# Both MLP layers of a four-layer transformer kernel, from one fp32 product to three fp32r products of high and low parts

## The chip, the cores and the metric

The kernel runs on one core of a Trainium2 chip. The time is the device time of one execution in microseconds (us), lower is better; the median of the runs of a kernel is compared.

A core has five engines with an instruction queue each: TensorE (PE, matrix products into the accumulator memory PSUM), VectorE (DVE), ScalarE (ACT), GpSimd (POOL) and SyncE (SP, which issues the DMAs here). They meet at semaphores only.

## The reference

`x` and a context have 8 batches of 512 tokens of 256 features, all in fp32. Four layers follow one another; the stages that the change touches are the two MLPs, at the end of layer 0 and of layer 2:

```python
# layer 0                                        # layer 2, the same form
x = x + self_attention(ln1(x))                   # 16 heads of 16
x = x + cross_attention(ln2(x), ctx)
h = gelu(ln3(x) @ fc_w.T + fc_b)                 # 256 -> 1024, exact Gelu
x = x + h @ proj_w.T + proj_b                    # 1024 -> 256
```

Layer 1 is a cross attention with quantized weights, layer 3 a causal attention with heads of 64.

## The kernel before

Everything stays on the chip: `X` holds all 8 batches (128 partitions = tokens of a tile, 4 tiles a batch, 256 columns). The program runs eight stages in order: SELF0, CROSS0, MLP0, CROSS1, SELF2, CROSS2, MLP2, SELF3. Between some of them, the MLP stages among them, all engines wait on `x_done` for the last batch of the stage before (L886, L1074, L1373, L1596).

An MLP stage loops over `NB` = 8 batches. Its first and last batch are written out, the six between are a loop on each engine. The weights of a stage (`W_even`, 128 x 4096 fp32: 2048 columns for the first layer, `wf`, 2048 for the second, `wp`) are loaded during the stage before.

- PE (`mlp`, L710 to L744). `turn(b)` transposes the normalized batch, 4 transposes of 128x128 into each of the banks `LA` and `LB`. `batch(b)` makes the first layer: for each of `NF` = 8 chunks `f` of 128 hidden units two products over the 256 features (`NC` = 2 halves `c`, 512 columns each) into `FR[f % 4]`, one of four PSUM banks, after the wait for the Gelu three chunks back. Then come the transposes of the next batch, then the wait for all eight Gelus, then the second layer: 4 token tiles x 8 chunks, 256 columns a product, into `OV[0]` and `OV[1]`. The records name `FR` as MX and ST, and `h1T` as V, since it lies in the memory of V.
- ACT (`mlp`, L983 to L1004). `turned(b)` evacuates LA and LB into `hT` with the layer norm's scale and shift; for each chunk one Gelu with bias from PSUM into `h1T` (128 x 8 x 512).
- DVE (`mlp`, L1200 to L1214). The layer norm's statistics of batch b+1 (4 `bn_stats`, 4 `bn_aggr`), then for both halves of the second layer `add_to_x`, `X` plus the PSUM bank.
- POOL (`mlp`, L1515 to L1528). `layer_norm` of batch b+1: scale (L1399), power (L1401), centring (L1407), product (L1412) into `XH`, the centring once the transposes of the batch before are done; then `add_bias` for batch b (L1418) once `add_to_x` is done. That operation also counts up `x_done`.

In time, a batch's second layer ends, DVE adds, POOL adds the bias and makes the next layer norm, while PE is in the first layer of the next batch.

fp32r is the 4-byte type that PE multiplies in rounded form. The attention stages use it for scores: `stk` holds high and low parts of queries and keys on 48 or 50 partitions, and SELF2 adds its mask by two products of `identr` with `mask_hi` and `mask_lo` on 128 partitions (L667 to L669). The two parts of that mask are made by L1367 (copy to fp32r) and L1369 (subtraction). All products are recorded under L529, all transposes here under L539. `hi` and `lo` (128 x 2 x 512 fp32r) belong to the attention stages and are free in an MLP stage, as is `stk`.

Of the kernel before, what the change touches and what calls it, by code (L numbers as in the profile page):

```python
# [8 lines left out]
F32 = mybir.dt.float32  # L9
# [6 lines left out]
P = 128  # L16
NB = 8
# [43 lines left out]
def program(nc, x_in, ctx_in, ctx_rows_in, masks_in, shapes_in, cols_in, rows_in, wts, out):  # L61
# [12 lines left out]
    with es:  # L74
# [69 lines left out]
        columns3 = Pr[:, 0, 0:2, :].rearrange("p a (k m) -> p (a k) m", m=P)  # L144

# [14 lines left out]
        def P3(qt, h):  # L160
# [34 lines left out]
            sem("fc_full"), sem("gelu_done"), sem("pr_full"), sem("pr_evac"), sem("ml_full"), sem("ml_evac"))  # L195
        bias3, later3_set, cols3_in, k3_apart = sem("bias3"), sem("later3_set"), sem("cols3_in"), sem("k3_apart")
# [61 lines left out]


# [267 lines left out]
        def _(pe):  # L527
# [182 lines left out]
            def mlp(s):  # L710
                m = MLP_NO[s]
                wf = W[s % 2][:, 0:2048].rearrange("p (c o) -> p c o", c=NC)
                wp = W[s % 2][:, 2048:4096].rearrange("p (f o) -> p f o", f=NF)
# [7 lines left out]
                def batch(b, more):  # L721
                    MB = NB * m + b
                    pe.wait_ge(ml_evac, 2 * (MB + 1))
                    for f in range(NF):
                        wait(pe, gelu_done, NF * MB + f - 3)
                        for c in range(NC):
                            last = mm(FR[f % 4][:, :], wf[:, c, P * f:P * f + P], hT[:, c, :], c == 0, c == NC - 1)
                        last.then_inc(fc_full, 1)
                    if more:
                        turn(b + 1)  # L730
                    pe.wait_ge(gelu_done, NF * (MB + 1))
                    for j in range(2):
                        wait(pe, pr_evac, 2 * (MB - 1) + j + 1)
                        for t in range(2):
                            tok = slice(P * (2 * j + t), P * (2 * j + t) + P)
# [5 lines left out]
                batch(0, True)  # L741
                with pe.Fori(1, NB - 1) as b:
                    batch(b, True)
                batch(NB - 1, False)  # L744
# [161 lines left out]
        def _(act):  # L906
# [76 lines left out]
            def mlp(s):  # L983
                m = MLP_NO[s]

                def turned(b):
                    for c, bank in enumerate((LA, LB)):
                        act.wait_ge(ml_full, 2 * (NB * m + b) + c + 1)
                        nc.scalar.activation(hT[:, c, :], bank[:, :], ACT.Identity, **scale_shift(s, c)).then_inc(ml_evac, 1)

                def batch(b, more):
# [5 lines left out]
                    if more:  # L997
                        turned(b + 1)

                turned(0)  # L1000
                batch(0, True)
                with act.Fori(1, NB - 1) as b:
                    batch(b, True)
                batch(NB - 1, False)  # L1004
# [79 lines left out]
        def _(dve):  # L1084
# [115 lines left out]
            def mlp(s):  # L1200
                m = MLP_NO[s]

                def batch(b, more):
                    if more:
                        layer_norm_x(NB * s + b + 1, b + 1)
                    for j in range(2):
# [4 lines left out]
                batch(0, True)  # L1211
                with dve.Fori(1, NB - 1) as b:
                    batch(b, True)
                batch(NB - 1, False)  # L1214
# [173 lines left out]
        def _(pool):  # L1388
# [126 lines left out]
            def mlp(s):  # L1515
                m = MLP_NO[s]

                def batch(b, more):
                    if more:
# [3 lines left out]

                layer_norm(NB * s, xt(0, 0, NT))
                batch(0, True)
                with pool.Fori(1, NB - 1) as b:
                    batch(b, True)
                batch(NB - 1, False)  # L1528
# [173 lines left out]
```

## Time and profile before

| | us |
|---|---|
| median of 3 runs (4552.29 to 4562.95) | 4558.77 |
| the profiled execution, its own time | 4563.0 |
| MLP0 stage, from `x_done` to `x_done` | 245.0 |
| MLP2 stage | 245.1 |

The profile is one execution, taken by the hardware profiler. PE is the matmul unit, PEld its weight loads, which are recorded apart. A fp32 product has two matmul records and two loads, a fp32r product one of each. Matmuls are pipelined and a record is longer than the step to the next, so what counts is the distance from start to start. A load that is needed at once starts with its product; otherwise loads run ahead. PEclk (the granted clock) is the share of full speed at which TensorE ran: 1.00 is 2.4 GHz, 0.50 is 1.2 GHz. "Idle before" is idle time of an engine ahead of a group and what ended it. A line of the timeline that merges several instructions gives the start of the first and the time to the end of the last.

### The profile page before, as it was taken

To read this page: it belongs to the slowest core of one execution; us is meant where nothing else is said; L and a number is where in the kernel's file an instruction comes from. 1 tells how busy PE (TensorE), PEld (TensorE's weight loads), DVE (VectorE), ACT (ScalarE), POOL (GpSimd) and SP (SyncE) were. 2 spreads that over 40 slices of the span, in tenths; PEclk is the share of its full clock that TensorE was granted. 3 is DMA by queue.
4 is the path that set the end of the run, shared out by engine and by line. 5 is a ranking of instruction groups with operands and counts; after the bars stand their busy time and mean duration, and the time that the engine had idled before them with its cause. 6 is when DMAs were issued, how large, how long until landed. Compare 5 with 4: busy or idle time off the path is not lost. (4 is left out here: it accounts for less than half of the span.)

```text
span 4563.0 us, 63561 instructions
## 1 busy us (share of the span) xinstructions
PE 4206.8 (92%) x20178; PEld 2005.3 (44%) x20178; DVE 2460.5 (54%) x6321; ACT 2386.1 (52%) x5045; POOL 1642.4 (36%) x1661
## 2 busy tenths in 40 slices
PE   6988899999796999999999999999797999999998
PEld 3333333333464333333333333333464555555555
DVE  4555567775013777776666667776011544444443
ACT  2444456666221666666666666666221555555553
POOL 2332321111221111236556541110221766666664
PEclk7888889999897899999999999999798999999999
DMA  4433334442001444433222234442000000000000
GB/s 94 81 64 61 62 66 98 78 78 50 16 0 32 97 79 74 76 58 74 51 52 50 48 62 96 72 76 55 27 0 28 6 1 10 11 10 11 10 6 10
DMA packets 135470, 219.98 MB, mean 48 GB/s; under 512 B 42736, under 2 KB 45168, under 8 KB 133488
## 3 DMA queue, kind: packets, MB, share of 16 engines
q1 hardware_dynamic: 135152, 216.02, 24.0%
q8 instruction: 165, 2.70, 0.3%
q14 instruction: 153, 1.25, 0.1%
HBM read 59.69 MB, written 5.51 MB: 14 GB/s over the span
## 5 line engine op out<-in xcount | busy, mean ns | idle before, releaser
L967 ACT ACTIVATE Pr<-ST 128x512 f32<-128x512 f32 (+3 forms) x2392 | 1249.3, 563 | 990.3 <-PE ST L529 907.2
L529 PE MATMUL ST<-stk 50*128 50x512 f32 (+3 forms) x2560 | 1075.8, 471 | 98.9 <-ACT Pr L967 86.3
L1169 DVE TENSOR_REDUCE mx<-MX 128x1 f32<-128x512 f32 x1056 | 699.7, 683 | 251.4 <-PE MX L529 250.0
L529 PE MATMUL MX<-stk 48*128 48x512 f32 (+3 forms) x1760 | 753.6, 463 | 23.7 <-issue 11.9
L1548 POOL TENSOR_SCALAR Pr<-Pr,mx 128x128 f32<-128x128 f32 (+3 forms) x512 | 548.4, 1083 | 384.1 <-DVE mx L1307 384.1
L529 PE MATMUL OV<-Pr,V 128*32 128x512 f32 (+3 forms) x4784 | 649.9, 618 | 2.6 <-ACT Pr L967 1.5
L529 PEld LDWEIGHTS MX<-stk 48*128 48x128 f32 x1760 | 316.9, 195 | 614.6 <-issue 265.5
L529 PEld LDWEIGHTS ST<-stk 50*128 50x128 f32 x2560 | 441.8, 194 | 275.1 <-ACT Pr L967 233.9
L1421 POOL CAST mhl<-mx 128x16 fp32r<-128x16 f32 x160 | 31.6, 197 | 1121.2 <-DVE mx L1169 1078.1
L529 PE MATMUL OV<-stk 48*128 48x512 f32 (+3 forms) x800 | 366.6, 458 | 57.2 <-DVE mx L1169 45.3
L1169 DVE TENSOR_REDUCE mx<-OV 128x1 f32<-128x512 f32 x480 | 324.8, 677 | 65.0 <-PE OV L529 64.1
L1162 DVE CUSTOM_DVE_ANT_0 MX<-MX,W_even 128x512 f32<-128x512 f32 x352 | 244.4, 699 | 150.9 <-PE MX L529 124.1
L529 PEld LDWEIGHTS OV<-stk 48*128 48x128 f32 x800 | 156.6, 196 | 350.7 <-DVE mx L1169 224.8
L1499 POOL TENSOR_TENSOR Pr<-Pr,W_odd 128x512 f32<-128x512 f32 x172 | 220.3, 1282 | 177.5 <-ACT Pr L967 177.4
L1036 ACT ACTIVATE Pr<-MX,mx 128x128 f32<-128x128 f32 (+3 forms) x256 | 134.9, 527 | 263.9 <-DVE mx L1301 263.4
L1418 POOL TENSOR_TENSOR X<-X,brow 128x1024 f32<-128x1024 f32 (+1 forms) x56 | 132.0, 2357 | 378.7 <-DVE X L1108 378.7
L1166 DVE CUSTOM_DVE_ANT_0 MX<-MX,later 128x128 f32<-128x128 f32 (+3 forms) x352 | 174.2, 511 | 170.5 <-PE MX L529 168.1
L1108 DVE TENSOR_TENSOR X<-OV,X 128x512 f32 (+1 forms) x32 | 22.1, 691 | 428.0 <-PE OV L529 428.0
L1316 DVE COPY PT<-OV 128x128 f32<-128x128 f32 (+3 forms) x256 | 125.5, 490 | 222.6 <-PE OV L808 222.6
L1301 DVE CUSTOM_DVE_ANT_0 MX<-MX,sums 128x128 f32<-128x128 f32 (+3 forms) x256 | 126.9, 496 | 212.4 <-PE ST L529 208.3
L529 PE MATMUL OV<-W_even,V 128*128 128x256 f32 x1024 | 225.2, 381 | 1.6 <-ACT V L995 1.6
L1506 POOL TENSOR_SCALAR_AFFINE_SELECT Pr<-Pr 128x512 f32<-128x512 f32 x128 | 81.3, 635 | 376.7 <-ACT Pr L967 376.7
(144 smaller groups left out, 7198.3 us busy)
## 6 DMA issues: line engine op xcount, KB each, us to landing
stk<-hi SPq DMA_DIRECT2D x640, 128.0 KB, 4.0
stk<-lo SPq DMA_DIRECT2D x320, 128.0 KB, 3.9
misc<-misc SPq DMA_DIRECT2D x160, 128.0 KB
sums<-spread SPq DMA_DIRECT2D x80, 256.0 KB
misc<-in_ctx_t SPq DMA_DIRECT2D x24, 512.0 KB, 6.6
W_even<-in_w SPq DMA_DIRECT2D x4, 1024.0 KB, 5.2
W_even<-in_w SPq DMA_DIRECT2D x2, 2048.0 KB, 10.5
XH<-in_ctx_rows SPq DMA_DIRECT2D x8, 512.0 KB, 3.9
```

Of the source, the lines that this page charges most:

```text
L529: return nc.tensor.matmul(o, l, r, start=start, stop=stop)
L967: nc.scalar.activation(pr_buffer(s, u, i)[:, h, q0:S], ST[h % 2][:, q0:S], func).then_inc(ex_done, 1)
L1036: nc.scalar.activation(P3(qt, h)[:, 0:k_n], S3[h][t % 2][:, 0:k_n], ACT.Exp, bias=low3[:, qt, h:h + 1], scale=-1.0, accum_out=total3[:, qt ...
L1162: nc.vector.tensor_tensor_reduce(bank[:, :], bank[:, :], mask_q[:, qt, :], 1.0, -3.0e38, ALU.add, ALU.max, m).then_inc(mx_red, 1)
L1166: nc.vector.tensor_tensor_reduce(bank[:, 0:k_n], bank[:, 0:k_n], later0[:, S - k_n:S], 1.0, -3.0e38, ALU.add, ALU.max, m).then_inc(mx_red, 1)
L1169: nc.vector.tensor_reduce(m, bank[:, :], AX.X, ALU.max).then_inc(mx_red, 1)
L1301: nc.vector.tensor_tensor_reduce(bank, bank, later3[:, S - k_n:S], 1.0, 3.0e38, ALU.add, ALU.min, low3[:, qt, h:h + 1]).then_inc(low3_done, 1)
L1316: nc.vector.tensor_copy(to, TP3[1][:, 0:P * (qt + 1)].rearrange("p (k n) -> p k n", n=P)).then_inc(tp3_evac[1], 1)
L1418: nc.gpsimd.tensor_tensor(xt(b, 0, NT), xt(b, 0, NT), bias, ALU.add).then_inc(x_done, 1)
L1499: nc.gpsimd.tensor_tensor(tile, tile, mask_k[:, i % 4, :], ALU.add).then_inc(pool_masked, 1)
L1506: nc.gpsimd.affine_select(tile, tile, [[0, G], [1, P]], ALU.is_ge, 0.0, 0, -1).then_inc(cleared, 1)
L1548: nc.gpsimd.tensor_scalar(tile, tile, inv3[:, qt, h:h + 1], None, ALU.mult).then_inc(nm3_done, 1)
```

## The change

All products of both MLP stages are taken from high and low parts. High part: the value rounded to fp32r; low part: value minus high part, rounded too. A product w·h becomes w_hi·h_hi + w_lo·h_hi + w_hi·h_lo in one PSUM sum; w_lo·h_lo is left out.

- PE: 6 products a chunk in the first layer (48 a batch in place of 16 in fp32), 96 in place of 32 in the second. In each group the products with the low activations come last, behind a wait of their own (`ml_lo`, `h1_lo_done`). The wait for all Gelus at once is replaced by waits for each chunk's high and low part in the first token tile. In batch 0 there are also waits for the weights' parts.
- ACT: at the start of a stage the high parts of the weights in 8 pieces of 512 columns (`split_weights`); per batch each of LA and LB is now evacuated twice, to `hi` and to `hT`.
- DVE: at the start the weights' low parts; per batch `split_hidden` for each chunk (a copy to `h1_hi`, a wait for it, a subtraction to `h1_lo`) between the layer norm's statistics and `add_to_x`, and `low_turned` (two subtractions) ahead of `add_to_x`.
- POOL: the same operations.
- Memory: `w_hi` and `w_lo` lie in `stk`, `h1_hi` in `misc`, `h1_lo` in `Pr`. All four loops over batches are written out.

```diff
+        w_hi = stk[:, 16:24, :].rearrange("p a n -> p (a n)")
+        w_lo = stk[:, 24:32, :].rearrange("p a n -> p (a n)")
+        h1_hi = nc.alloc_sbuf_tensor_at("h1_hi", [P, NF, S], F32R, offset=misc_at)
+        h1_lo = nc.alloc_sbuf_tensor_at("h1_lo", [P, NF, S], F32R, offset=pr_at)
+        def weight_cut(k):
+            if k < 4:
+                return [(E * k + c * 1024, E) for c in range(NC)]
+            return [(2048 + 512 * (k - 4), 512)]
...
@@ PE, mlp
-                def batch(b, more):
-                    pe.wait_ge(ml_evac, 2 * (MB + 1))
+                def batch(b):
+                    pe.wait_ge(ml_hi, 2 * (MB + 1))
                     for f in range(NF):
+                        cut = slice(P * f, P * f + P)
                         wait(pe, gelu_done, NF * MB + f - 3)
+                        if b == 0 and f % 2 == 0:
+                            pe.wait_ge(wf_hi_done, 8 * m + f // 2 + 1)
+                            pe.wait_ge(wf_lo_done, 8 * m + f // 2 + 1)
                         for c in range(NC):
-                            last = mm(FR[f % 4][:, :], wf[:, c, P * f:P * f + P], hT[:, c, :], c == 0, c == NC - 1)
+                            mm(FR[f % 4][:, :], wf_hi[:, c, cut], hi[:, c, :], c == 0, False)
+                            mm(FR[f % 4][:, :], wf_lo[:, c, cut], hi[:, c, :], False, False)
+                        if f == 0:
+                            pe.wait_ge(ml_lo, 2 * (MB + 1))
+                        for c in range(NC):
+                            last = mm(FR[f % 4][:, :], wf_hi[:, c, cut], lo[:, c, :], False, c == NC - 1)
                         last.then_inc(fc_full, 1)
...
-                    pe.wait_ge(gelu_done, NF * (MB + 1))
+                    if b == 0:
+                        pe.wait_ge(wf_hi_done, 8 * (m + 1))
+                        pe.wait_ge(wf_lo_done, 8 * (m + 1))
                     for j in range(2):
                         wait(pe, pr_evac, 2 * (MB - 1) + j + 1)
                         for t in range(2):
                             for f in range(NF):
-                                last = mm(OV[j][:, E * t:E * t + E], h1T[:, f, tok], wp[:, f, :], f == 0, f == NF - 1)
+                                if j == 0 and t == 0:
+                                    pe.wait_ge(h1_hi_done, NF * MB + f + 1)
+                                mm(bank, h1_hi[:, f, tok], wp_hi[:, f, :], f == 0, False)
+                                mm(bank, h1_hi[:, f, tok], wp_lo[:, f, :], False, False)
+                            for f in range(NF):
+                                if j == 0 and t == 0:
+                                    pe.wait_ge(h1_lo_done, NF * MB + f + 1)
+                                last = mm(bank, h1_lo[:, f, tok], wp_hi[:, f, :], False, f == NF - 1)
                         last.then_inc(pr_full, 1)
@@ ACT, mlp
+                def split_weights():
+                    act.wait_ge(w_in[s], 16)
+                    for k in range(8):
+                        cut = weight_cut(k)
+                        nc.scalar.activation(w_part(w_hi, cut), w_part(W[s % 2], cut), ACT.Copy).then_inc(wf_hi_done, 1)
                 def turned(b):
                     for c, bank in enumerate((LA, LB)):
+                        nc.scalar.activation(hi[:, c, :], bank[:, :], ACT.Identity, **scale_shift(s, c)).then_inc(ml_hi, 1)
                         nc.scalar.activation(hT[:, c, :], bank[:, :], ACT.Identity, **scale_shift(s, c)).then_inc(ml_evac, 1)
@@ DVE, mlp
+                def weights_low():
+                    for k in range(8):
+                        cut = weight_cut(k)
+                        dve.wait_ge(wf_hi_done, 8 * m + k + 1)
+                        nc.vector.tensor_tensor(w_part(w_lo, cut), w_part(W[s % 2], cut), w_part(w_hi, cut).bitcast(F32),
+                                                ALU.subtract).then_inc(wf_lo_done, 1)
+                def low_turned(b):
+                    for c in range(NC):
+                        dve.wait_ge(ml_evac, 2 * (NB * m + b) + c + 1)
+                        nc.vector.tensor_tensor(lo[:, c, :], hT[:, c, :], hi[:, c, :].bitcast(F32), ALU.subtract).then_inc(ml_lo, 1)
+                def split_hidden(b, f):
+                    at = NF * (NB * m + b) + f
+                    dve.wait_ge(gelu_done, at + 1)
+                    nc.vector.tensor_copy(h1_hi[:, f, :], h1T[:, f, :]).then_inc(h1_hi_done, 1)
+                    dve.wait_ge(h1_hi_done, at + 1)
+                    nc.vector.tensor_tensor(h1_lo[:, f, :], h1T[:, f, :], h1_hi[:, f, :].bitcast(F32),
+                                            ALU.subtract).then_inc(h1_lo_done, 1)
+                def batch(b):
+                    if b + 1 < NB:
                         layer_norm_x(NB * s + b + 1, b + 1)
+                    for f in range(NF):
+                        split_hidden(b, f)
+                    if b + 1 < NB:
+                        low_turned(b + 1)
                     for j in range(2):
                         dve.wait_ge(pr_full, 2 * (NB * m + b) + j + 1)
                         add_to_x(b, j, OV[j][:, :].rearrange("p (t n) -> p t n", t=2), pr_evac)
                 layer_norm_x(NB * s, 0)
+                weights_low()
+                low_turned(0)
+                for b in range(NB):
+                    batch(b)
```

## Rows read from the trace of the kernel before

**Rows 1.** The page, part 1: busy us (share) x instructions.
```profile
PE 4206.8 (92%) x20178; PEld 2005.3 (44%) x20178; DVE 2460.5 (54%) x6321; ACT 2386.1 (52%) x5045; POOL 1642.4 (36%) x1661
```

**Rows 2.** Stretches: length, busy PE PEld DVE ACT POOL (count), PEclk, DMA share, GB/s.
```profile
1172.03:1417.00 244.97, 232.89 (x832) 154.10 (x832) 24.38 (x80) 56.17 (x81) 59.02 (x40) 0.97 0.02 6
1213.00:1385.08 172.08, 172.08 (x625) 114.57 (x624) 18.14 (x60) 41.00 (x60) 44.23 (x30) 1.00 0.00 0
3240.50:3485.60 245.10, 232.73 (x832) 154.13 (x832) 24.40 (x81) 56.17 (x81) 59.19 (x41) 0.97 0.02 9
```

**Rows 3.** Waits in MLP0: who <- for whom: total us, times, longest.
```profile
DVE X L1108 <- PE OV L529: 214.1, 16, 26.7
...
PE LA L539 <- POOL XH L1412: 10.5, 1, 10.5
```

**Rows 4.** Timeline of batch 1 of MLP0: start, us, engine, instruction, xcount.
```profile
1213.00 3.60 PE L529 MATMUL MX<-hT,W_even 128*128 128x512 f32 x8
...
1213.97 2.35 POOL L1418 TENSOR_TENSOR X<-X,brow 128x1024 f32<-128x1024 f32 x1 [28.72 <-DVE X L1108]
...
1215.12 0.36 DVE L1096 BATCH_NORM_AGGREGATE mv<-st 128x2 f32<-128x6 f32 x4
...
1216.43 3.60 PE L529 MATMUL ST<-hT,W_even 128*128 128x512 f32 x8
...
1217.92 1.90 POOL L1407 TENSOR_TENSOR XH<-X,mv 128x1024 f32<-128x1024 f32 x1 [0.29 <-POOL rstd L1401]
...
1226.73 0.60 PE L539 MATMUL LA<-ident,XH 128*128 128x128 f32 x4
1227.17 0.60 PE L539 MATMUL LB<-ident,XH 128*128 128x128 f32 x4
1227.77 0.91 PE L529 MATMUL OV<-W_even,V 128*128 128x256 f32 x3
```

**Rows 5.** Timeline of SELF2: the two mask products, the second one's load.
```profile
2306.00 0.50 PE L529 MATMUL ST<-stk,identr 128*128 128x512 f32 x1
...
2306.34 0.40 PE L529 MATMUL ST<-stk,identr 128*128 128x512 f32 x1
...
2306.11 0.19 PEld L529 LDWEIGHTS ST<-stk,identr 128*128 128x128 f32 x1
```

**Rows 6.** Timeline of SELF0, causal: fp32r products of 256 columns, a load.
```profile
180.54 0.33 PE L529 MATMUL MX<-stk 48*128 48x256 f32 x1
180.71 0.33 PE L529 MATMUL OV<-stk 48*128 48x384 f32 x1
...
180.59 0.19 PEld L529 LDWEIGHTS OV<-stk 48*128 48x128 f32 x1
```

**Rows 7.** Lines: durations min/median/max in ns; DVE operations from SBUF to SBUF.
```profile
L1219 DVE TENSOR_SCALAR W_odd<-W_odd x3: 416/427/622, 568.8 to 2608.0; 128x512 f32<-128x512 f32 x3
L1367 DVE CAST stk<-W_odd x1: 1222/1222/1222, 1936.9 to 1936.9; 128x2048 fp32r<-128x2048 f32 x1
L1369 DVE TENSOR_TENSOR stk<-W_odd,stk x1: 2291/2291/2291, 1938.2 to 1938.2; 128x2048 fp32r<-128x2048 f32 x1
```

**Rows 8.** Timeline, DVE beside POOL: program start and SELF2's end.
```profile
5.66 2.46 DVE L1352 CAST identr<-ident 128x128 fp32r<-128x128 f32 x1 [5.66 <-issue]
0.97 7.07 POOL L1582 MEMSET stk<- 32x4096 f32 x2
...
2608.01 0.62 DVE L1219 TENSOR_SCALAR W_odd<-W_odd 128x512 f32<-128x512 f32 x1
2607.08 1.27 POOL L1499 TENSOR_TENSOR Pr<-Pr,W_odd 128x512 f32<-128x512 f32 x1 [1.17 <-ACT Pr L967]
```

**Rows 9.** Timeline of MLP0: first product, last batch's second layer.
```profile
1181.28 0.78 ACT L989 ACTIVATE hT<-LB,cols 128x512 f32<-128x512 f32 x1
1182.11 5.89 PE L529 MATMUL MX<-hT,W_even 128*128 128x512 f32 x8 [0.87 <-ACT hT L989]
...
1399.76 14.08 PE L529 MATMUL OV<-W_even,V 128*128 128x256 f32 x64 [0.78 <-ACT V L995]
```

More of the change, by code:

```diff
@@ L257, in wq, with w_part @@
             return W[s % 2][:, 512 * m:512 * m + 512].rearrange("p (c o) -> p c o", c=NC)
+        def weight_cut(k):
+            if k < 4:
+                return [(E * k + c * 1024, E) for c in range(NC)]
+            return [(2048 + 512 * (k - 4), 512)]
+        def w_part(w, cut):
+            at, n = cut[0]
+            if len(cut) == 2:
+                return w[:, 0:2048].rearrange("p (c o) -> p c o", c=NC)[:, :, at:at + n]
+            return w[:, at:at + n]
         def stages(u):
@@ L711, in mlp @@
                 m = MLP_NO[s]
-                wf = W[s % 2][:, 0:2048].rearrange("p (c o) -> p c o", c=NC)
-                wp = W[s % 2][:, 2048:4096].rearrange("p (f o) -> p f o", f=NF)
+                wf_hi, wf_lo = (w[:, 0:2048].rearrange("p (c o) -> p c o", c=NC) for w in (w_hi, w_lo))
+                wp_hi, wp_lo = (w[:, 2048:4096].rearrange("p (f o) -> p f o", f=NF) for w in (w_hi, w_lo))
                 def turn(b):
@@ L996, in batch @@
                                              bias=cols[:, at:at + 1]).then_inc(gelu_done, 1)
-                    if more:
+                    if b + 1 < NB:
                         turned(b + 1)
+                split_weights()
                 turned(0)
[L1001 to L1004, printed above, removed]
+                for b in range(NB):
+                    batch(b)
             def layer3(s):
@@ L1201, in mlp, with batch @@
                 m = MLP_NO[s]
-                def batch(b, more):
-                    if more:
+                def weights_low():
[15 more added lines that the diff above has]
+                                            ALU.subtract).then_inc(h1_lo_done, 1)
+                def batch(b):
+                    if b + 1 < NB:
                         layer_norm_x(NB * s + b + 1, b + 1)
+                    for f in range(NF):
+                        split_hidden(b, f)
+                    if b + 1 < NB:
+                        low_turned(b + 1)
                     for j in range(2):
@@ L1210, in mlp @@
                 layer_norm_x(NB * s, 0)
[L1211 to L1214, printed above, removed]
+                weights_low()
+                low_turned(0)
+                for b in range(NB):
+                    batch(b)
             def scale_queries(s, w, scale):
@@ L1516, in mlp @@
                 m = MLP_NO[s]
-                def batch(b, more):
-                    if more:
+                layer_norm(NB * s, xt(0, 0, NT))
+                for b in range(NB):
+                    if b + 1 < NB:
                         layer_norm(NB * s + b + 1, xt(b + 1, 0, NT), ml_full, 2 * (NB * m + b + 1))
@@ L1522, in batch @@
                     add_bias(s, b)
[L1524 to L1528, printed above, removed]
             def layer3(s):
```

14 lines of the change are left out of this document (6 added, 8 removed).

## Prediction

> **What bounds the kernel now.** I read four views in this order. The page's busy line says TensorE (PE) is busy 92% of the span [rows 1], an average over eight stages, so it settles nothing for the two that change. The table by stretch gives those: the MLP stages last 245.0 and 245.1 us, PE busy 233 of each, and the six middle batches of the first show 172.08 us busy of 172.08 at granted clock 1.00 [rows 2]. There is no gap at all. The waits of that stage agree: DVE waits for PE for 214 us in all; PE's one long wait is 10.5 us for the first layer norm [rows 3]. So a batch costs what PE's instructions cost, 172.08 / 6 = 28.68 us, and there are 16. The timeline of one batch takes it apart [rows 4]. First layer: 8 records in 3.43 us (1213.00 to 1216.43), two records to an fp32 product, so 0.858 us for 512 columns, and 16 of them make 13.7. Eight transposes and the step to the second layer take 1.04 (1226.73 to 1227.77). Second layer: 64 records (32 products of 256 columns) take 13.8 (14.08 with the drain). Beside them ACT is busy 41.00 / 6 = 6.8 us, POOL 7.4 and DVE 3.0: all idle for most of a batch.
>
> **What the change does to PE.** One fp32 product (two records of 0.429 us at 512 columns) becomes three fp32r products of one record each. Their price is not in the MLP stages, so it comes from the nearest rows. 512 columns on all 128 rows: two mask products in attention start at 2306.00 and 2306.34; the first had to wait for its own weights, whose load takes 0.107 (the next load starts at 2306.11) [rows 5]. That leaves 0.232 us streamed, where half an fp32 record is 0.214. I take 0.234 with the step; 0.216, half a record with the step, is the other end. First layer: 8 chunks x 2 x 3 = 48 products, 48 x 0.234 = 11.2 us (10.4 at the fast end) against 13.7.
>
> 256 columns: a load of 128 columns now lies behind every 0.11 us of streaming. In the causal stage a load starts at 180.59 and its product at 180.71, 0.12 later, while the product before it (256 columns, recorded at 180.54 but with its weights there only at 180.59) streamed [rows 6]. The load ran beside the product and the pair took 0.12. The transposes are the other end: four loads and four products in 0.44 (1226.73 to 1227.17), 0.110 each [rows 4]. I take 0.12, as that row has the fp32r type. Second layer: 4 token tiles x 8 x 3 = 96 products, 11.5 us (10.5) against 13.8. With 0.95 for the transposes (the loop's own step left out) PE needs 11.2 + 0.95 + 11.5 = 23.7 us a batch (21.9 at the fast ends). The loops go as well: a batch is now written out.
>
> **What it adds elsewhere.** ACT: two more evacuations of 0.78 a batch [rows 9], 8.4 us in all, under PE's 23.7; they are queued behind the eighth Gelu and are needed only by the next batch, 11.5 us later: nothing. DMA: nothing. POOL's work stays at 7.4 us. DVE gets a copy and a subtraction for each of 8 hidden chunks. A one-input SBUF operation of 512 columns is 0.42 us, the fp32r copy of 2048 is 1.22, so 0.15 of each is fixed; the subtraction of 2048 is 2.29, so one of 512 is 2.14 / 4 + 0.15 = 0.69 [rows 7]; with the handover between them a chunk takes 1.09. Two low parts of the activations (1.4) come behind, hidden under the second layer. A batch's DVE work is 3.0 + 8.7 + 1.4 = 13.1 us, well under 23.7; a chunk's 1.09 is under PE's 1.40 a chunk. On busy time alone, DVE hides.
>
> It is the place that matters. The eight splits can't start before the two layer-norm steps of the next batch (DVE free 2.48 us after the batch's start, 1215.48 less 1213.00), and in just this time POOL works: bias 0.97 to 3.32, two small operations, centring 4.92 to 6.82, and a product of the same length [rows 4]. The trace shows that DVE and POOL hold each other up. At the start a cast of 128x128 took 2.46 us and ended 0.08 after POOL's memset, and a 0.42 us operation became 0.62 beside a POOL tensor_tensor that ended at 2608.35 [rows 8]. For the subtraction with two SBUF inputs beside POOL there is no row. Bounds: no hold-up, or a full one like the copy's. I take the full one, since the copy is the nearest row and both bring two SBUF streams into DVE at once.
>
> Turn by turn, from the batch's start (after a hand-over a copy needs 0.28, as in the 2608 row, a subtraction 0.55 by the same 0.14 off): POOL's bias to 3.3; copy 0 to 3.6; POOL's first small one to 3.8; subtraction 0 to 4.3; the second (about 1.0) to 5.3; copy 1 to 5.6; centring to 7.5; subtraction 1 to 8.1; POOL's product to 10.0 (before PE wants it at 11.2); copy 2 and subtraction 2 to 10.95; then five chunks of 1.09 alone, so the high part of the eighth chunk is there at 15.7. PE reaches the product that waits for it at 11.2 + 0.95 + 14 x 0.12 = 13.9. It waits 1.8, and then 82 products of 0.12 are left: 15.7 + 9.8 = 25.5 us a batch. The eighth low part (16.4) is not late, since PE asks for it 9 products later (16.8). If only the copies are held, the same count gives 14.4 for that high part and 24.2 a batch. If nothing is, 23.7.
>
> The Trainium skill ("SBUF — State Buffer", SBUF: two separate sides) says that DVE and GpSimd share one port pair as an exclusive lock for a whole instruction, taken by DVE also for two SBUF inputs against a GpSimd operation that reads SBUF. The rows on the copies agree (0.62 against 0.42); by that rule it would be 25.5, by busy time alone 23.7.
>
> **Start and end of a stage.** The first layer norm's 10.5 us on POOL is the one time when PE waits [rows 9]. ACT copies the weights' high parts there (eight of at most 0.78, from 1172.0), each ready ahead of DVE. DVE's 8 subtractions are interleaved with POOL's four operations, three or four ahead of POOL's end, 0.55 each: 2.0 us later, between 0 and 2.5. The first product then waits for both high evacuations, and a hidden copy to hT now stands between them: +0.78 (ACT 0.78 each; 1182.11 was right behind the second). I take 2.8 us a stage. The low activations are asked for four products later and are ready 1.5 later (0.78 and 0.69); the clock is low there (8 records in 5.89 us in place of 3.60 [rows 4, 9]), so four products last about as long. The last batch has no transposes and no layer norm: now 14.68 to the second layer (with 0.78 waiting for Gelu) plus 13.8 and some drain, 28.6 [rows 9]; afterwards 11.2 + 11.5 = 22.8 (the eighth high part at 12.6 is in time for 12.9). It saves 5.8.
>
> **Sum.** 14 batches x (28.68 - 25.5) = 44.5; 2 last ones x 5.8 = 11.6; less 2 x 2.8 = 5.6: 50.5 us. The profiled execution's own 4563.0 becomes 4512.5. It is at the top of the three runs, 4.2 above their median, so the forecast for the median is 4508 us.
>
> **Rivals.** (1) Little or no hold-up between DVE and POOL: 24.2 a batch gives 14 x 4.5 + 11.6 - 3 = 71 us, 4488; with 23.7, 78 us, 4480. For it: no row shows two-input operations colliding. Against: the copies do. (2) The products run at the fast ends, 0.216 and 0.110, and nothing is held up: 21.9 a batch, 14 x 6.8 + 2 x 7.7 - 3 = 108, 4451. Against: the two mask products of rows 5 start 0.34 apart, not 0.32. (3) Slower: the weight loads of the second layer become the bound. Before, a load of 0.19 lay behind 0.215 of streaming; now it lies behind 0.116. If it does not run beside the product, a step is 0.107 + 0.116 = 0.223, the second layer 21.4 us, a batch 33.6, and the kernel 16 x 4.9 + 3 = 81 us slower, 4640. It decides from a step of (28.68 - 12.15) / 96 = 0.172 on. Against: rows 4 and 6, where load and product overlap. The Trainium skill ("TensorE: Matmul & The Clock Gate", Measured speedup vs the span model) says that a load overlaps running matmuls only where the row groups differ. Here they never do; both layers would pay it, 38.6 a batch and about 4720 us. The trace speaks against it: full-row transposes with a load each follow every 0.110 us. (4) The hold-up is worse, or the one-pass product at 256 columns steps at 0.16 to 0.17 because of its waits (16 of them stand in the first token tile): 27.5 to 28.5 a batch, 4536 to 4550, no change at its end. Against: fulfilled waits at chunk boundaries cost nothing now (records step on at 0.43).
>
> **How the numbers follow.** Forecast with the full hold-up (4495 to 4525): 0.52. Rival 1 (4474 to 4495): 0.27. Rival 2 (under 4474): 0.08. Rival 4: 0.08, of it 0.03 within no change. Rival 3: 0.05. The range reaches from rival 1's lower end to some way into rival 4: 4466 to 4530; outside lie rival 2, rival 3 and most of 4, under 2 in 10. What a measurement can tell from no change is 0.2%, 9 us: faster 0.92, same 0.03, slower 0.05.
>
> **What would show it.** A middle batch of 25.5 us, not 23.7 or 28.7. First-layer products starting 0.232 to 0.236 apart, second-layer ones 0.12. One wait of PE a batch, some 1.8 us, in the first token tile of the second layer, for the high part of the eighth chunk. DVE copies and subtractions stretched to 1 to 2 us while POOL's bias and layer norm run, and 0.42 and 0.69 afterwards; POOL's product ending 10 us after the batch's start. Layers outside the MLP stages unchanged. Wrong would be: a step of 0.17 or more in the second layer, a clock under 1.00 in the middle batches, or a wait of PE on ACT.

## The result, and the profile after

| | before | after |
|---|---|---|
| median (range) | 4560.86 (4552.29 to 4577.34), 4 runs | 4483.74 (4481.09 to 4504.7), 4 runs |
| the profiled execution, span of its core | 4563.0 | 4479.3 |
| MLP0 / MLP2, from `x_done` to `x_done` | 245.0 / 245.1 | 208.4 / 208.5 |
| a middle batch | 28.68 | 24.36 |

The ratio of the times is 0.9839, 95% interval 0.981 to 0.9869. The kernel is 77 us (1.6%) faster by the medians, where 51 were forecast. All times below are in us.

The table by stretch of the kernel after (length, busy PE, PEld, DVE, ACT, POOL with counts, granted clock, DMA share, GB/s): MLP0, one middle batch, MLP2. It answers to [rows 2].

```profile
1177.60:1386.00 208.40, 192.25 (x1216) 173.38 (x1216) 136.76 (x232) 71.24 (x105) 67.88 (x40) 0.96 0.02 7
1238.46:1262.81 24.35, 23.79 (x154) 21.46 (x153) 16.50 (x28) 8.20 (x12) 8.61 (x5) 1.00 0.00 1
3191.30:3399.80 208.50, 192.31 (x1216) 173.43 (x1216) 136.76 (x233) 71.24 (x105) 67.88 (x40) 0.97 0.03 12
```

Each stage is 36.6 shorter, 73.2 together; the two profiled spans are 83.7 apart. The other 10.5 lie in the attention stages, whose code is the same. The batch is no longer all PE: it is busy 23.79 of 24.35, and DVE has gone from 3 to 16.5 us a batch, POOL from 7.4 to 8.6 with the same work.

The waits of PE on DVE from the start of MLP0 into its last batch (who on whom, total, times, longest; batches 1 to 6 have one of PE each):

```profile
PEld OV L549 <- DVE h_hi L1262: 5.7, 12, 0.8
PE OV L549 <- DVE h_hi L1262: 3.4, 6, 0.6
```

So there is one wait of PE a batch, on the copy to `h1_hi`. The timeline of batch 1 shows where. First PE (start, us, instruction, count): the first products of the first layer, the transposes, the first token tile of the second layer.

```profile
1214.09 1.09 PE L549 MATMUL MX<-hi,stk 128*128 128x512 f32 x4
...
1225.00 0.60 PE L559 MATMUL LA<-ident,XH 128*128 128x128 f32 x4
...
1225.79 2.17 PE L549 MATMUL OV<-stk,h_hi 128*128 128x256 f32 x14
1228.52 0.51 PE L549 MATMUL OV<-stk,h_hi 128*128 128x256 f32 x2 [0.56 <-DVE h_hi L1262]
1228.86 1.12 PE L549 MATMUL OV<-stk,h_lo 128*128 128x256 f32 x8
1229.82 2.08 PE L549 MATMUL OV<-stk,h_hi 128*128 128x256 f32 x16
```

The first layer starts at 1214.09 and the transposes at 1225.00: 48 products in 10.91, 0.2273 each. The transposes take 0.79 (to 1225.79). In the second layer 8 products take 0.96 (1228.86 to 1229.82), 0.120 each. Fourteen products would end at 1225.79 + 14 x 0.12 = 1227.47; the fifteenth runs at 1228.52, 1.05 late. The profile calls 0.56 of this idle, because the last record before it outlasts its step. Then DVE and POOL in the same batch:

```profile
1215.06 2.40 POOL L1486 TENSOR_TENSOR X<-X,brow 128x1024 f32<-128x1024 f32 x1 [17.26 <-DVE X L1152]
1216.49 1.26 DVE L1262 CAST h_hi<-V 128x512 fp32r<-128x512 f32 x1
1217.92 1.46 POOL L1469 TENSOR_TENSOR rstd<-rstd,mhalf 128x4 f32<-128x4 f32 x1
1218.39 0.42 DVE L1262 CAST h_hi<-V 128x512 fp32r<-128x512 f32 x1
1218.84 0.69 DVE L1264 TENSOR_TENSOR h_lo<-V,h_hi 128x512 fp32r<-128x512 f32 x1
1219.45 2.18 POOL L1475 TENSOR_TENSOR XH<-X,mv 128x1024 f32<-128x1024 f32 x1
1219.45 0.42 DVE L1262 CAST h_hi<-V 128x512 fp32r<-128x512 f32 x1
1219.91 2.27 DVE L1264 TENSOR_TENSOR h_lo<-V,h_hi 128x512 fp32r<-128x512 f32 x1
1221.71 2.22 POOL L1480 TENSOR_TENSOR XH<-XH,rstd 128x1024 f32<-128x1024 f32 x1
1222.10 2.11 DVE L1262 CAST h_hi<-V 128x512 fp32r<-128x512 f32 x1
1224.25 0.69 DVE L1264 TENSOR_TENSOR h_lo<-V,h_hi 128x512 fp32r<-128x512 f32 x1
...
1228.05 0.42 DVE L1262 CAST h_hi<-V 128x512 fp32r<-128x512 f32 x1
```

Read it in pairs. The first copy (0.42 alone) takes 1.26 and ends at 1217.75, 0.29 after POOL's bias. A subtraction with two SBUF inputs (0.69 alone) takes 2.27 beside POOL's centring, a copy 2.11 beside POOL's product: each ends 0.3 to 0.55 after POOL does. All three began after POOL's operation. The copy that began with the centring, at 1219.45, took 0.42, and there the centring took 2.18 in place of 1.90. But beside POOL's power operation on 4 columns (1217.92 to 1219.38) DVE runs at full pace, a copy in 0.42 and a subtraction in 0.69; there POOL is the one that takes longer, 1.46 where the same operation took 1.04 before the change. The eighth copy ends at 1228.47, 14.4 after the batch's start.

### The profile page after: what moved, and what is told of

Same layout as the page of the kernel before. It is cut to its first block and busy times, and to the rows that moved or that the text cites. A ratio compares the mean times of both kernels' runs of the same rounds, so it can differ in the third digit from the quotient of the medians.

```text
span 4479.3 us, 64827 instructions
## 1 busy us (share of the span) xinstructions
PE 4109.2 (92%) x20946; PEld 2036.5 (45%) x20946; DVE 2682.3 (60%) x6625; ACT 2418.5 (54%) x5093; POOL 1661.2 (37%) x1661
## 5 line engine op out<-in xcount | busy, mean ns | idle before, releaser
L1384 DVE COPY PT<-OV 128x128 f32<-128x128 f32 (+3 forms) x256 | 125.6, 491 | 224.2 <-PE OV L844 224.2
L1486 POOL TENSOR_TENSOR X<-X,brow 128x1024 f32<-128x1024 f32 x56 | 132.6, 2368 | 277.4 <-DVE X L1152 277.4
L549 PE MATMUL MX<-QK 64*128 64x128 f32 (+3 forms) x512 | 206.5, 483 | 0.7 <-ACT Pr L1080 0.7
L549 PE MATMUL ST<-QK 64*128 64x128 f32 (+3 forms) x512 | 206.5, 483 | 0.0
## 6 DMA issues: line engine op xcount, KB each, us to landing
W_even<-in_w SPq DMA_DIRECT2D x2, 2048.0 KB, 10.1
```

The costliest lines, as they stand in the source:

```text
L549: return nc.tensor.matmul(o, l, r, start=start, stop=stop)
L1384: nc.vector.tensor_copy(to, TP3[1][:, 0:P * (qt + 1)].rearrange("p (k n) -> p k n", n=P)).then_inc(tp3_evac[1], 1)
L1486: nc.gpsimd.tensor_tensor(xt(b, 0, NT), xt(b, 0, NT), bias, ALU.add).then_inc(x_done, 1)
```

## The experiments

Two theories are to be told apart. A: after the change a batch is set by DVE's chain up to the eighth high part, and this is longer than DVE's own work because POOL's wide operations hold DVE; PE's own work is 23.3. B: PE's products or their weight loads set the batch, and the wait of 0.56 is a symptom. "Theory" in the quoted expectations means these where nothing else is said there. The ratios are to the kernel before, run beside each experiment. A middle batch and the length of a stage (between the ends of POOL's last bias additions) come from the profiled execution. Where the granted clock stays at 1.00 they repeat within 0.1 us from batch to batch, while whole runs of one kernel differ by 15 to 30.

| kernel | time, median or one run | stages | middle batch |
|---|---|---|---|
| after | 4483.74 | 208.4 / 208.5 | 24.36 |
| e1, POOL on one column | 4473.45 | 200.0 / 199.7 | 23.30 |
| e2, high part by ACT | 4476.46 | 202.1 / 202.1 | 23.30 |
| e9, power twice (one run) | 4501.9 | 209.8 / 209.6 | 24.38 |
| e3, two products in layer 1 (one run) | 4477.03 | 209.9 / 206.7 | 24.36 |
| e8, copies twice (one run) | 4577.62 | 240.1 / 240.7 | 28.5 to 29.5 |
| e4, half the columns in layer 2 (one run) | 4508.4 | 209.6 / 219.1 | 23.64 |
| e5, first layer only (one run) | 4497.53 | 222.7 / 222.9 | 25.78 |
| e6, second layer only (one run) | 4526.78 | 224.1 / 224.2 | 26.12 |
| e7, e2 and another order | 4465.92 | 201.1 / 201.2 | 23.30 |

**POOL's wide operations taken away.**

```diff
-                        layer_norm(NB * s + b + 1, xt(b + 1, 0, NT), ml_full, 2 * (NB * m + b + 1))
+                        rows_scale(N)
...
+                        one = XH[:, 0:1, 0:1]
+                        nc.gpsimd.tensor_tensor(one, xt(b + 1, 0)[:, :, 0:1], mv[:, 0:1, 0:1], ALU.subtract).then_inc(ln_pool, 1)
...
+                        nc.gpsimd.tensor_tensor(one, one, rstd[:, 1:2, 0:1], ALU.mult).then_inc(xh_ready, 1)
...
-                    add_bias(s, b)
+                    nc.gpsimd.tensor_tensor(one_x, one_x, brow[:, s % 2, 1:2, 0:1], ALU.add).then_inc(x_done, 1)
```

> In the MLP batches POOL's layer norm of the next batch and its bias work on one column in place of 1024; their semaphores stay, so the normalized rows and the bias are left out of the result. Theory A (DVE and POOL hold each other up, and this alone makes PE wait): no DVE copy over 0.45 us and no subtraction over 0.72, PE's wait of 1.1 us in the second layer is gone, a middle batch goes from 24.36 to 23.2 us; over 14 batches and two stage starts (POOL's first layer norm stays as it is) about 16 us less than the changed kernel. Rival B (DVE is simply too slow, 1.09 us a chunk behind the layer norm's statistics): the wait stays at 1.1, the time within 3 us.

Measured: 4473.45 (4458.09 to 4488.36), ratio 0.9823 (0.979 to 0.9856). The copies' and the subtractions' line, each for the kernel after (first two) and for e1 (durations min/median/max in ns), and a middle batch of e1:

```profile
L1262 DVE CAST h_hi<-V x128: 412/420/2116, 1192.9 to 3385.9; 128x512 fp32r<-128x512 f32 x128
L1264 DVE TENSOR_TENSOR h_lo<-V,h_hi x128: 691/693/2270, 1193.3 to 3386.3; 128x512 fp32r<-128x512 f32 x128
```
```profile
L1262 DVE CAST h_hi<-V x128: 393/427/430, 1183.2 to 3363.6; 128x512 fp32r<-128x512 f32 x128
L1264 DVE TENSOR_TENSOR h_lo<-V,h_hi x128: 691/693/695, 1183.7 to 3364.1; 128x512 fp32r<-128x512 f32 x128
1227.90:1251.20 23.30, 23.30 (x155) 21.35 (x154) 13.19 (x28) 8.20 (x12) 2.52 (x5) 1.00 0.00 1
```

With POOL's wide operations gone no DVE operation is stretched, PE has no gap, and the batch is 23.30. That is A's number. The 1.06 between 24.36 and 23.30 is the price of the hold-up. The two stages are 17.2 shorter together, where 16 were expected; 4.3 of it is the last bias addition of each stage, 0.19 in place of 2.34, which comes of what e1 leaves out.

**The copies taken off DVE.** POOL's work stays; ACT, which sat idle, makes the high part with a second Gelu.

```diff
+                        nc.scalar.activation(h1_hi[:, f, :], FR[f % 4][:, :], ACT.Gelu,
+                                             bias=cols[:, at:at + 1]).then_inc(h1_hi_done, 1)
...
-                    nc.vector.tensor_copy(h1_hi[:, f, :], h1T[:, f, :]).then_inc(h1_hi_done, 1)
```

> The high part of each hidden chunk is written by ACT, by a second Gelu from the same PSUM bank to fp32r; DVE keeps the subtraction alone. Nothing is left out. Theory A: ACT goes to 8 x 1.34 + 2.7 = 13.4 us a batch, under PE's 23.2; DVE needs 0.63 a chunk, the eighth high part is there 1.6 us after its products, PE's wait is gone: 23.2 us a batch, about 16 us less than the changed kernel in all, 4468 for the median, and faster than both kernels. Rival B2 (ACT becomes the bound): two Gelus of 0.67 a chunk against 1.36 of PE's first layer is close; if PE waits for a bank at each chunk, the first layer grows from 10.9 to 11 to 12 us and the gain shrinks to between 0 and 16 us.

Measured: 4476.46 (4470.04 to 4486.55), ratio 0.9814 (0.9788 to 0.984). A middle batch of e2:

```profile
1248.60:1271.90 23.30, 23.30 (x155) 21.35 (x154) 12.83 (x20) 12.81 (x20) 8.19 (x5) 1.00 0.00 1
```

The same 23.30, with POOL untouched: shortening DVE's chain does what narrowing POOL's operations does. ACT's time in a batch grew from 8.20 to 12.81 and PE does not wait for it, so rival B2 is out. The two stages are 12.7 shorter together, not the 16 expected: 12 times 1.06, and nothing in the first and last batches.

**Which POOL operation holds DVE?** The chain was 1.3 shorter than forecast, and the rows above lay that on the power operation, which the forecast had counted as holding DVE. Here it is made twice.

```diff
                         pool.wait_ge(ln_pool, 3 * N + 1)
+                        nc.gpsimd.tensor_tensor(sums[:, 0, 0:NT], rstd[:, 0, :], mhalf[:, :], ALU.pow)
                         nc.gpsimd.tensor_tensor(rstd[:, 1, :], rstd[:, 0, :], mhalf[:, :], ALU.pow).then_inc(ln_pool, 1)
```

> In batches 1 to 7 of both MLP stages POOL makes its power operation of 4 columns twice (the second result goes to free memory), so 14 operations of 1.04 to 1.46 us more; nothing is left out. Theory A, the small POOL operation does not hold DVE, only the bias, centring and product of 1024 columns do: POOL's chain ends 1.1 to 1.5 us later (11.0 to 11.4 after the batch's start in place of 9.84), DVE puts one more copy and subtraction of 0.42 and 0.69 into the gap, and the eighth high part stays at +14.4 (within 0.5, as another subtraction or copy falls on the start of each wide operation). PE waits up to 0.5 for XH ahead of the transposes, and less by as much for the eighth part. Middle batch 24.4 (24.1 to 24.8). Theory B, every POOL operation holds DVE for its whole length, and the 1.3 us that the chain is shorter than forecast come from elsewhere: the eighth part moves by the operation's length, to +15.6 or +15.9, and the batch is 25.5 to 25.8.

Measured: one run, 4501.9; a middle batch 24.38. POOL and DVE in batch 1 (which starts at 1222.78):

```profile
1226.60 1.45 POOL L1593 TENSOR_TENSOR sums<-rstd,mhalf 128x4 f32<-128x4 f32 x1
1228.03 1.05 POOL L1594 TENSOR_TENSOR rstd<-rstd,mhalf 128x4 f32<-128x4 f32 x1
1229.16 1.90 POOL L1475 TENSOR_TENSOR XH<-X,mv 128x1024 f32<-128x1024 f32 x1
1231.13 1.96 POOL L1480 TENSOR_TENSOR XH<-XH,rstd 128x1024 f32<-128x1024 f32 x1
...
1228.13 0.42 DVE L1262 CAST h_hi<-V 128x512 fp32r<-128x512 f32 x1
1228.59 0.69 DVE L1264 TENSOR_TENSOR h_lo<-V,h_hi 128x512 fp32r<-128x512 f32 x1
1229.20 2.14 DVE L1262 CAST h_hi<-V 128x512 fp32r<-128x512 f32 x1
1231.37 2.26 DVE L1264 TENSOR_TENSOR h_lo<-V,h_hi 128x512 fp32r<-128x512 f32 x1
```

The added 1.05 us of POOL cost the batch 0.02. (The stages are 1.4 and 1.1 longer, by batch 0, where in MLP0 the low clock lasted longer: the same first layer took 13.8, not 12.5.) The eighth copy ends 14.38 after the start, as before. Only POOL's wide operations hold DVE, and now it is a copy beside the centring and a subtraction beside the product, with the same 2.1 to 2.3. POOL's chain ended only 0.5 later (1233.09, +10.3), not the 1.1 to 1.5 expected, as centring and product were hardly held by DVE this time (1.90 and 1.96 in place of 2.18 and 2.22): both began before DVE's operation. So length in time alone does not hold DVE: the two powers together take 2.5, the centring 1.9. e1 says the same of the kind of operation: its subtraction and product of one column (0.38 and 0.19) stretch no copy beyond 0.43. That leaves the width; a wide power operation was not run.

**PE work taken away: does the batch follow?** The 16 products of a batch with the low parts of the first layer's weights are left out.

```diff
-                            mm(FR[f % 4][:, :], wf_lo[:, c, cut], hi[:, c, :], False, False)
```

> In the first layer the products of the weights' low parts are left out (32 products a batch in place of 48). Theory A (DVE's splits, held up by POOL, set the batch's end): the first layer takes 7.3 us in place of 10.9, but the eighth high part still comes 14.4 us after the batch's start, so PE's wait grows from 1.1 to about 4.7 and a middle batch stays at 24.2 us (0.1 to 0.2 less); in all 10 to 14 us less, from the first and last batches. Rival (the number of products sets the time): 20.7 us a batch and about 58 us less in all.

Measured: one run, 4477.03; the middle batch is 24.36, to the hundredth what it was with all products (two batches, in which the granted clock fell, took 1.6 more). PE in one of them, around the transposes and the first token tile:

```profile
1273.37 0.63 PE L559 MATMUL LA<-ident,XH 128*128 128x128 f32 x4 [2.54 <-POOL XH L1479]
...
1274.19 2.00 PE L549 MATMUL OV<-stk,h_hi 128*128 128x256 f32 x12
1276.75 0.51 PE L549 MATMUL OV<-stk,h_hi 128*128 128x256 f32 x2 [0.56 <-DVE h_hi L1261]
1277.81 0.51 PE L549 MATMUL OV<-stk,h_hi 128*128 128x256 f32 x2 [0.56 <-DVE h_hi L1261]
```

The work that is gone, 16 x 0.227 = 3.6, came back as 2.54 of waiting for POOL's `XH` and more for the last high parts. That is A. The two stages gained only 0.3 together, where 10 to 14 were expected: batch 0 is 0.3 shorter and the last batch 1.3, since PE waits for high parts there too, and in MLP0 the fallen clock took 3.2 back. The expectation had also missed the first of these waits: with a shorter first layer PE is at the transposes before POOL has made the next layer norm, 9.84 after the batch's start. So 9.84 is the next floor behind DVE's chain, and the change has 10.91 - 9.84 = 1.07 of room above it.

**The chain made longer.** A second, unused copy ahead of each.

```diff
+                    nc.vector.tensor_copy(sums[:, f % 2, :], h1T[:, f, :])
                     nc.vector.tensor_copy(h1_hi[:, f, :], h1T[:, f, :]).then_inc(h1_hi_done, 1)
```

> The changed kernel with one more DVE copy of each hidden chunk, to memory that nobody reads. Theory A (DVE's chain sets the middle batches): each adds its step of 0.34 us, those beside POOL partly hidden: the eighth high part comes 2.0 to 2.7 us later and a middle batch goes from 24.36 to between 26.4 and 27.1 us. Rival (PE's wait is for something else, the semaphore or ACT): 24.4.

Measured: one run, 4577.62, so slower than the kernel before; batches of 28.5 to 29.5. The eighth high part came 17.2 after the start (1225.78 to 1242.97), 2.8 later, where A had 2.0 to 2.7. But the batch grew by 4 to 5, where A had 2.0 to 2.7 too. PE in the second layer of batch 1, and the stretches (as in the first table) from 1240.00 to 1248.00 and from there on:

```profile
1240.22 0.50 PE L549 MATMUL OV<-stk,h_hi 128*128 128x256 f32 x2 [0.90 <-DVE h_hi L1263]
1241.62 0.80 PE L549 MATMUL OV<-stk,h_hi 128*128 128x256 f32 x2 [0.90 <-DVE h_hi L1263]
1243.02 0.80 PE L549 MATMUL OV<-stk,h_hi 128*128 128x256 f32 x2 [0.60 <-DVE h_hi L1263]
1243.61 1.91 PE L549 MATMUL OV<-stk,h_lo 128*128 128x256 f32 x8
1245.32 3.28 PE L549 MATMUL OV<-stk,h_hi 128*128 128x256 f32 x16
1248.43 1.12 PE L549 MATMUL OV<-stk,h_lo 128*128 128x256 f32 x8
...
1240.00:1248.00 8.00, 6.28 (x27) 5.78 (x28) 4.79 (x10) 0.26 (x1) 0.00 (x0) 0.58 0.01 2
1248.00:1255.00 7.00, 7.00 (x60) 7.00 (x59) 0.69 (x1) 0.00 (x0) 0.00 (x0) 1.00 0.00 0
```

PE waited three times, 0.6 to 0.9 each, for the sixth to eighth high part. The granted clock fell to its lower level (1.2 GHz) during the second wait: it is 0.85 in the 0.6 us from 1240.80 and 0.50 from 1241.40 on. 24 products then took 4.82 (1243.61 to 1248.43), 0.20 each, not 0.12. So A had the chain nearly right and the batch wrong by the clock. Here the longer waits cost more than their own length; the one wait a batch of the kernel after does not, its middle batches show 1.00. That the waits brought the clock down is likely from the order in time, but not shown: in e4 below it also falls without a longer wait.

**What a product of fewer columns costs.** The second layer with 128 of 256 columns; half of its output is left out.

```diff
-                            tok, bank = ..., OV[j][:, E * t:E * t + E]
+                            tok, bank = ..., OV[j][:, E * t:E * t + P]
...
-                                mm(bank, h1_hi[:, f, tok], wp_lo[:, f, :], False, False)
+                                mm(bank, h1_hi[:, f, tok], wp_lo[:, f, 0:P], False, False)
```

> The second layer computes 128 of its 256 columns (the other half of each output is left out); number of products and weight loads as before. If the step of 0.120 us of its products is set by the load of 128 weight columns alone, it stays 0.120 and the layer 12.65 us with its wait. If streaming 256 columns sets it (0.116) and the load lies just under it (0.107), it becomes 0.107 to 0.110 and the layer 11.5, about 16 us less in all. If loads are no limit at all, it becomes 0.06 and the layer 6.9 us, about 90 us less.

Measured: one run, 4508.4; the second layer of batch 0, which has no wait, took 10.75, 0.112 a product. Its timeline, then one stretch of batch 1:

```profile
1195.68 1.98 PE L549 MATMUL OV<-stk,h_hi 128*128 128x128 f32 x16
1197.50 1.06 PE L549 MATMUL OV<-stk,h_lo 128*128 128x128 f32 x8
...
1223.40:1236.00 12.60, 12.60 (x62) 12.60 (x60) 0.69 (x1) 0.00 (x0) 0.00 (x0) 0.50 0.00 0
```

Half the columns save 0.008 of 0.120. At 128 columns something that goes with each product and not with its columns is the bound, the weight load by all appearance (0.107 in the prediction), and it is just under the price at 256 columns. Hence loads do run beside the products of 256 columns. The batch of 23.64 is A once more: 14.4 to the eighth part and 82 products of 0.112. The stretch from 1223.40 shows what was not foreseen: a clock of 0.50 while PE issued without a gap. It began 2.5 after PE's usual wait for the eighth high part (0.62, up to 1220.87), which the batches at full clock have too. It came in batch 1 of MLP0 and twice in MLP2, not in the five others of MLP0, and it is why the stages are longer than the batch of 23.64 makes them: together 11.8 more than the kernel after's, where 16 less were expected. Its cause stays open.

**One layer alone.** In e5 the second layer keeps its fp32 products, in e6 the first.

```diff
# e5
-                                mm(bank, h1_hi[:, f, tok], wp_hi[:, f, :], f == 0, False)
...
+                                last = mm(OV[j][:, E * t:E * t + E], h1T[:, f, tok], wp[:, f, :], f == 0, f == NF - 1)
# e6
-                            mm(FR[f % 4][:, :], wf_hi[:, c, cut], hi[:, c, :], c == 0, False)
...
+                            last = mm(FR[f % 4][:, :], wf32[:, c, cut], hT[:, c, :], c == 0, c == NC - 1)
```

> Only the first layer is made of high and low parts; the second is the fp32 one of before and DVE has no splits of hidden chunks. By the step of the products (0.227 us x 48 against 0.429 x 32) the first layer is 10.9, the second 13.9: 25.6 us a batch, PE without a wait, 3.1 less than before; about 48 us less than before over both stages.

> Only the second layer is made of high and low parts; the first is the fp32 one of before, 13.7 us. Theory A (the wait comes of the short first layer): the eighth Gelu comes 14.6 us after the batch's start, its high part at 15.1, and PE asks for it at 13.7 + 0.9 + 1.7 = 16.3: no wait, the second layer 11.6, a batch 26.1 us. The two parts alone then save 3.1 + 2.6 = 5.7 a batch, together they saved 4.3, and the difference is the wait. Rival (PE waits for each new high part whatever comes before): 12.7 for the second layer, 27.2 a batch.

Measured: 4497.53 and 4526.78, one run each. A middle batch of each, e5 first:

```profile
1230.61:1256.39 25.78, 25.78 (x122) 22.01 (x121) 4.36 (x12) 8.20 (x12) 7.41 (x5) 1.00 0.00 1
```
```profile
1247.98:1274.10 26.12, 26.12 (x138) 18.41 (x137) 14.72 (x26) 6.84 (x10) 8.08 (x5) 1.00 0.00 1
```

The first layer alone saves 28.68 - 25.78 = 2.90 a batch, the second 28.68 - 26.12 = 2.56, with no gap in PE in either. Together they would save 5.46; the change saves 4.32. The missing 1.14 is the wait, but for 0.08 (28.68 - 23.30 = 5.38): with both layers shortened PE is at the eighth chunk 13.38 after the start, with e6's fp32 first layer only at 13.73 + 0.79 + 14 x 0.12 = 16.2, when the high part has long been there. The second layer's gain is what the hold-up eats into. e6's rival, a wait whatever comes before (27.2), is out.

**The version built from this.** e2, and at the start of a stage DVE makes the low parts of the weights only after POOL's first layer norm, and ACT evacuates both `hi` before both `hT`.

```diff
+                    for c, bank in enumerate((LA, LB)):
                         nc.scalar.activation(hT[:, c, :], bank[:, :], ACT.Identity, **scale_shift(s, c)).then_inc(ml_evac, 1)
...
-                weights_low()
+                dve.wait_ge(xh_ready, NB * s + 1)
+                weights_low(range(4))
                 low_turned(0)
+                weights_low(range(4, 8))
```

> The version with the high part by ACT, and two changes at the start of a stage: DVE's low parts of the weights come after the first layer norm, so that they don't meet POOL's four operations, and ACT evacuates both high parts of the activations before the full ones. Theory A: POOL's first layer norm takes 5.3 us again in place of 6.3, the first product comes 0.67 earlier for the order: 1.5 to 1.7 us a stage less, a middle batch stays at 23.3 us, an MLP stage goes from 202.1 to 200.5 and the kernel is some 3 us faster than that version (too little for the medians, visible in the stage). Rival (the start of a stage is set by the weights' parts): nothing gained, since the low parts now come later.

Measured: 4465.92 (4445.66 to 4471.05), ratio 0.9793 (0.9766 to 0.982), the lowest median of all. Its stage start:

```profile
1183.31 4.26 ACT L1027 ACTIVATE stk<-W_even 128x512 fp32r<-128x512 f32 x8 [19.31 <-POOL X L1490]
...
1190.58 1.08 PE L559 MATMUL LA<-ident,XH 128*128 128x128 f32 x4 [10.45 <-POOL XH L1484]
...
1193.39 2.07 PE L549 MATMUL MX<-hi,stk 128*128 128x512 f32 x4 [0.87 <-ACT hi L1033]
```

The first product is 10.1 behind `x_done` (1183.31 to 1193.39), as before the change, where the kernel after needs 11.6: the 1.5 is back. The stage, though, is only 1.0 shorter than e2's, and less than the 1.5 to 1.7 expected, since the first layer of batch 0 now takes 13.06 in place of 12.62. Its first products with the activations' low part start 2.06 after the first product, in e2 1.87, and their load waits 0.7 for `lo`. The other 0.25 may be the clock, still low there, whose rise also differs between kernels with the same first layer (12.5 and, in e9, 13.8); it was not taken apart. Against the kernel after the profiled stages are 7.3 shorter each, 14.6 in all. The medians are 17.8 apart, but the two were not run beside each other, and the intervals of their ratios just touch (0.981 to 0.9869, 0.9766 to 0.982). It is the stages that show the gain.

## Why the prediction was right, and where it was not

The forecast was 4508 in a range of 4466 to 4530, the measured median 4483.74. Sign, mechanism and place held: one wait of PE a batch, in the first token tile, for the eighth high part, because DVE and POOL hold each other up. But the time, a batch of 24.36 and a saving of 73 in the stages, is what rival 1 gave (24.2 a batch, 71, 4488), though not for its reason. The central sum got 51 of the 77. That the time lies inside the range is owed in part to its width, which took in rival 1's, and some of the 77 is scatter outside the stages. By the steps:

- **The hold-up (the term that failed).** The forecast let every POOL operation hold DVE and had the eighth high part at +15.7; it came at +14.4. Held were the copy beside the bias (1.26), and two operations beside centring and product (2.27 and 2.11). Rival 1's condition, that a subtraction with two inputs is not held, is wrong: 2.27 against 0.69. What was over-counted is POOL's small power operation. During its 1.46 DVE made a copy and most of two subtractions, so that at +10.9 it had finished four chunks, where the turn-by-turn count had three. e9 isolates it: doubled, it moves nothing. PE's wait, forecast at 1.8, is 1.05. The rest is that a chunk alone takes 1.06 and not 1.09.
- **PE's own work.** First layer 10.91, forecast 11.2 (0.227 a product, under the 0.232 to 0.236 that it was to show); transposes 0.79, forecast 0.95; second layer 96 x 0.12 = 11.5, as forecast. 23.3 in all, 0.4 less; but a middle batch does not gain by it, since the chain sets its end: 14.4 to the eighth part and 82 products of 0.12 make 24.2, of the 24.36.
- **Batch 0.** The sum gave it the 3.18 of the others; it saved 30.89 - 24.92 = 5.97 (1182.11 to 1213.00 [rows 4, 9], now 1189.17 to 1214.09). Its first layer is slow from the low clock (12.5), so PE is late at the second layer and waits for nothing: 11.6. This was left out of the sum, 2.8 a stage.
- **Start of a stage.** +1.5, forecast +2.8 (0 to 2.5, and 0.78). POOL's first layer norm lost 0.9 to DVE's subtractions, not 2.0 (PE's wait 11.4 after, 10.5 in [rows 3]), and the evacuation between the two high ones cost 0.6. e7 takes both back.
- **Last batch.** 22.5 where 22.8 was forecast: 10.9 + 11.5 (1360.27 to 1371.17, then 96 x 0.12), a saving of 6.1, not 5.8.
- **The sum again.** For a stage: 6 x 4.32 = 25.9, 5.97, 6.1, less 1.5: 36.5, and 36.6 were measured. The forecast of 25.3 for a stage is short by 6 x 1.14 = 6.8 (hold-up), 2.8 (batch 0), 1.3 (start) and 0.3 (last batch), 11.2.
- **From the stages to the run.** The other 10.5 of the 83.7 is scatter of the attention stages, no gain of the change. Their share of the span is 4072.9 before and 4062.4 after, but it runs from 4050 (e5) to 4095 (e8) in the experiments, none of which touches them. One profiled execution can't price anything there. The traces show that length and granted clock go together: the cross attention of layer 2 (the stage before MLP2) takes 489.4 at 0.91 before and 469.5 at 0.96 after, and over all eleven kernels from 469.4 at 0.96 (e5) to 492.2 at 0.90 (e8), the longer the lower the clock. Why the clock differs there from one execution to the next stays open.
- **Rival 2** (0.216 and 0.110 a product) is out: 0.227 and 0.120. **Rival 3** (the load does not run beside the product, 0.223 a step) is out by 0.120. The Trainium skill ("TensorE: Matmul & The Clock Gate", The mechanism) would have a load overlap running products only where row groups differ. The trace does not agree: all 96 products of the second layer have a load of their own on all rows and follow every 0.120 us, and e4's every 0.112. **Rival 4** did not come in this kernel, but e8 is the same mechanism with a longer chain: 28.5 to 29.5, up to 1.0 past the 28.5 it was given, since it left out the clock.

The Trainium skill ("SBUF — State Buffer", SBUF: two separate sides) has an exclusive lock on the shared port pair, also for a DVE operation with two SBUF inputs against a GpSimd operation that reads SBUF. The trace agrees for wide POOL operations: 2.27 in place of 0.69. For the power operation of 4 columns it does not: copies and subtractions pass beside it in 0.42 and 0.69.

## What to carry to other kernels

Fp32 products taken as three one-pass products brought a batch from 28.68 to 24.36 here, and what remained to be had hung on who makes the high and low parts: put them on an engine that is idle and that the others do not hold up (here ACT, whose second Gelu took 0.69 every time, for 23.30 a batch), before trimming PE. Where DVE and GpSimd work at the same time, follow them operation by operation, count a hold for each wide operation of the other that has already begun and none for the tiny ones, and look at which instruction of the bound engine asks for the last result. Judge such a change by the length of a stage or a batch in the trace, which repeat within 0.1 us, since whole runs of one kernel differ by 15 to 30.

## What was not expected of the hardware

- A one-pass fp32r product steps at 0.227 us for 512 columns, 0.120 for 256 and 0.112 for 128, each with its own load of 128 columns. An fp32 product of 512 columns steps at 0.858 (two records of 0.429), so the three that replace it (0.68) save a fifth.
- A DVE subtraction with two SBUF inputs is held by a wide POOL operation as fully as a copy (2.26 and 2.27 us in place of 0.69), and POOL by DVE in turn (centring 1.90 to 2.18, power 1.04 to 1.46). Between wide operations, the one that begins second is held. A POOL power operation on 4 columns (1.04 to 1.46 us) does not hold DVE, nor does one on one column in e1 (0.19 to 0.44).
- The granted clock fell to 0.50 during the second of three waits of 0.6 to 0.9 us in e8, and in e4 in some batches for 12.6 us and more with PE issuing without a gap, in others of the same kernel not at all.
